# A layered conditional network on one core: raw differences, cut order and transfer order around the gated unit changed

## The reference, cut to what matters

```python
def lora_add(base, inp, A, B):
    t = jnp.einsum('bri,bni->bnr', A[0][ids], inp)
    return base + jnp.einsum('bor,bnr->bno', B[0][ids], t) * SCALE
gate = lora_add(x @ W_gate.T, x, A_gate, B_gate)
up   = lora_add(x @ W_up.T,   x, A_up,   B_up)
act  = silu(gate) * up
x    = x + lora_add(act @ W_down.T, act, A_down, B_down)
```

## Time and profile before

| | |
|---|---|
| median of 3 runs | 2181.67 us (2180.75 to 2182.43) |
| profiled execution | 2176.47 us, its span 2174.8 us |
| PE busy in the span | 2086.6 us (96%), 10432 matmuls |
| DVE, ACT, POOL busy | 1605.5, 969.6, 115.2 us |
| mean granted TensorE clock | 0.993 of full |
| 662 to 720 us (rows, half unit, start of unit 1, stage 0) | PE busy 45.00 of 58 us, clock 0.91 |
| 1165 to 1230 us (end of the units, first panels, stage 0) | PE busy 59.92 of 65 us, clock 0.97 |
| 1430 to 1480 us (half unit and start of unit 1, stage 1) | PE busy 47.39 of 50 us, clock 0.97 |
| 1915 to 1975 us (end of the units, first panels, stage 1) | PE busy 53.42 of 60 us, clock 0.97 |

### The profile page before, as it was taken

How to read it: one execution, slowest core, us unless ns; L and a number is a source line. 1 busy time by engine, 2 the same in 40 slices (tenths; PEclk the granted TensorE clock), 3 DMA queues, 4 the chain that set the end, 5 groups by cost and what they waited for, 6 DMA issues and landing times.

```text
span 2174.8 us, 34185 instructions
## 1 busy us (share of the span) xinstructions
PE 2086.6 (96%) x10432; PEld 1774.5 (82%) x10432; DVE 1605.5 (74%) x2132; ACT 969.6 (45%) x1268; POOL 115.2 (5%) x167
## 2 busy tenths in 40 slices
PE   2998999999998899999999999999999999999998
PEld 2998888888887788888888888888888888877887
DVE  7777999999997887878785347367878787743433
ACT  2222888788885334343333225333334333323222
POOL 3110000000005230000000000000000000000000
PEclk9999999999999999999999999999999999999999
DMA  5999999989997673434334995443333333364543
GB/s 194 377 360 358 351 358 362 342 339 353 362 349 257 189 206 102 109 95 110 92 96 148 272 247 178 164 135 93 108 97 105 100 100 105 89 199 154 184 155 126
DMA packets 258274, 441.49 MB, mean 203 GB/s; under 512 B 146934, under 2 KB 151222, under 8 KB 238006
## 3 DMA queue, kind: packets, MB, share of 16 engines
q1 hardware_dynamic: 245206, 410.79, 57.3%
q0 software_dynamic: 10848, 29.91, 4.2%
q10 hardware_dynamic: 2176, 0.26, 0.1%
HBM read 400.74 MB, written 63.73 MB: 214 GB/s over the span
## 4 chain that ended last, share of the span: by engine, by line
PE 84%; DVE 7%; DMA 3%; issue 2%; ACT 2%; POOL 1%; DVEq 0%; SPq 0%; ACTq 0%; POOLq 0%
PE ps L1937 19%; PE ps L1938 19%; PE ps L1939 19%; PE ps L1881 6%; PE ps L1883 6%; PE ps L1882 6%; PE ps L1857 3%; PE ps L2016 2%; PE ps L2015 2%; PE ps L1890 1%; DMA wraw<-in_wd 1%; PE ps L2051 1%; DMA wraw<-picked_bd 1%; PE ps L2052 1%; DMA W<-in_w 1%
## 5 line engine op out<-in xcount | busy, mean ns | idle before, releaser
L1937 PE MATMUL ps<-rows,oph 128*128 128x512 f32 x1196 | 468.9, 392 | 10.6 <-ACT tmp L855 8.4
L1938 PE MATMUL ps<-rows,oph 128*128 128x512 f32 x1196 | 468.1, 391 | 0.0
L1939 PE MATMUL ps<-rows,opl 128*128 128x512 f32 x1196 | 466.3, 390 | 0.0
L1389 DVE TENSOR_TENSOR wl<-W,wh 128x2048 fp32r<-128x2048 f32 x152 | 342.2, 2283 | 5.8 <-ACT wh L791 5.7
L1473 DVE TENSOR_TENSOR tmp<-ps,tmp 128x512 f32<-128x512 f32 (+1 forms) x340 | 234.1, 689 | 131.8 <-PE ps L2016 66.9
L1470 DVE TENSOR_TENSOR wdl<-wraw,wdh 128x1024 fp32r<-128x1024 f32 x92 | 112.5, 1224 | 274.1 <-ACT wdh L855 274.1
L791 ACT ACTIVATE wh<-W 128x2048 fp32r<-128x2048 f32 x152 | 290.5, 1914 | 37.3 <-DMA W<-in_w 34.0
L1937 PE MATMUL ps<-acb_h,wdh 128*128 128x512 f32 (+1 forms) x736 | 282.1, 383 | 12.4 <-DVE wdl L1470 7.0
L1938 PE MATMUL ps<-acb_l,wdh 128*128 128x512 f32 (+1 forms) x736 | 281.0, 382 | 0.0
L1939 PE MATMUL ps<-acb_h,wdl 128*128 128x512 f32 (+1 forms) x736 | 280.8, 382 | 0.0
L1937 PEld LDWEIGHTS ps<-rows,oph 128*128 128x128 f32 x1196 | 225.9, 189 | 55.6 <-issue 7.7
(11 more groups left out here) (222 smaller groups left out, 2831.9 us busy)
## 6 DMA issues: line engine op xcount, KB each, us to landing
W<-in_w SPq DMA_DIRECT2D x152, 1024.0 KB, 6.1
raw<-in_wgu SPq DMA_DIRECT2D x168, 256.0 KB, 2.7
wraw<-in_wd SPq DMA_DIRECT2D x84, 512.0 KB
toep<-kpad SPq DMA_DIRECT2D x32, 1024.0 KB, 8.8
lraw<-picked_b SPq DMA_DIRECT2D x88, 256.0 KB, 4.0
raw<-kept_acts SPq DMA_DIRECT2D x88, 256.0 KB, 3.4
kept_acts<-tmp SPq DMA_DIRECT2D x84, 256.0 KB, 2.3
picked_b<-in_lora_b POOLq DMA_DIRECT2D x32, 352.0 KB, 4.6
```

Of the source, the lines that this page charges most:

```text
L1389: V.tensor_tensor(out=wl[:, c], in0=W[:, c], in1=wh[:, c].bitcast(F32), op=ALU.subtract).then_inc(w_lo, 1)
L1937: mm(to, lhsT=wh, rhs=mh, start=start, stop=False)
L1938: mm(to, lhsT=wh, rhs=ml, start=False, stop=False)
L1939: return mm(to, lhsT=wl, rhs=mh, start=False, stop=stop)
```

## The change

1. POOL keeps the raw difference T3; T4 (`second_half(0)` minus T2) goes to DVE, behind the first `ranks_part`.
2. Stage 0, ACT: an empty sigmoid loads the activation table early; `ranks_hi(0)`, then the cut of A11, stand before `ranks_projected`, both of whose halves now run together; T3 is cut next. DVE correspondingly: T4, the cut of T2, `ranks_lo(0)`, the cut of A11, then both `ranks_cut`.
3. Both stages, in the half unit: `copy_p1`, `ranks_hi` and `down_ranks_hi` of unit 1 go ahead of the last cuts; the halves' products, `ranks_lo(1)` and `down_ranks_lo(0)` stand ahead of the cuts of T3, S3, A22, T4, S4 on DVE. Unit 1 is written out ahead of the loop, which starts at 2 now.
4. Both stages, `first_panels`: of panel 1, output 0 goes ahead of `project_down`, and outputs 1 to 3 instead of 0 to 5 stand before the wait for `td_added`; outputs 4 to 7 come after outputs 6 and 7 of panel 0.
5. SP: the residual rows come in four parts of 512 KB, at panels 5, 9, 13, 17 of the stage's first tile and 4, 8, 12, 16 of its second, instead of 2 MB at panel 4 and 2 MB at panel 6 of the first; the 36 row loads come two a panel at panels 4 to 21 instead of three a panel at 8 to 19. A wait for the third sum is added ahead of a quarter's load.

```diff
+            def load_residual(tile, part):
+                if part == 0:
+                    sp.wait_ge(unit_step, at_step(tile // 2, FT, 1))
+                    sp.wait_ge(x_saved[tile // 2], 16)
+                mine = slice(2 * part, 2 * part + 2)
...
-                    if at == 4:
-                        load_residual(2 * st)
-                    if at == HALF_AT:
-                        load_residual(2 * st + 1)
-                    if 8 <= at < 20 and st == 0:
-                        load_rows(1, (at - 8) // 3, (at - 8) % 3)
+                    if at in (5, 9, 13, 17):
+                        load_residual(2 * st, at // 4 - 1)
+                    if at < 22 and st == 0:
+                        load_rows(1, 2 * (at - 4))
+                        load_rows(1, 2 * (at - 4) + 1)
...
-            pool.wait_ge(t_raw, 2)
-            pool.wait_ge(ap_lo, 2 * GR)
-            pool.tensor_tensor(out=by_rows(LO[T4]), in0=second_half(0), in1=by_rows(LO[T2]),
-                               op=ALU.subtract).then_inc(t4_raw, 1)
...
+                copy_p1(st, 1)
+                ranks_hi(st, 1)
+                down_ranks_hi(st, 0, at_step(st, 0, AD))
                 act.wait_ge(evict, emptied(st, 0, V_ACT0))
                 copy(ahl[0:HALF, 0, 0], s0[0:HALF]).then_inc(act_hi, 1)
...
                 ranks_part(st, 0)
+                if st == 0:
+                    dve.wait_ge(t_raw, 2)
+                    sub(by_rows(rraw[LO[T4]][:]), rows_in(0, 1), by_rows(rraw[LO[T2]][:])).then_inc(t4_raw, 1)
+                    dve.wait_ge(t4_raw, 1)
+                    operand_lo(T2, rraw[LO[T2]][:], 11)
+                    ranks_lo(st, 0)
                 ranks_part(st, 1)
+                if st == 0:
+                    lo(st, 1, A11)
                 ranks_cut(st, 0)
...
-                        project_down(st, FT - 1)
                     else:
-                        down(tile, tile * NPAN + 1, 1, range(6))
+                        down(tile, tile * NPAN + 1, 1, (0,))
+                        project_down(st, FT - 1)
+                        down(tile, tile * NPAN + 1, 1, (1, 2, 3))
                 pe.wait_ge(td_added, 2 * st + 2)
                 down(tile, tile * NPAN, 0, (6, 7), start=True).then_inc(panel_done, 1)
-                down(tile, tile * NPAN + 1, 1, (6, 7)).then_inc(panel_done, 1)
+                down(tile, tile * NPAN + 1, 1, (4, 5, 6, 7)).then_inc(panel_done, 1)
```

More of the change, by code:

```diff
@@ L347, in build @@
         tile_done = sem("tile_done")
-        resid_in = sem("resid_in")
+        resid_in = [sem(f"resid_in{j}") for j in range(2)]
         d_added = sem("d_added")
@@ L510, in next_quarters @@
                 load_quarter(2, u, 2)
+                sp.wait_ge(sums, u * 4 + (st * 4 * (FT - 1) + 3))
                 for k, slot in ((0, A11), (1, A12), (3, A22)):
@@ L981, in half_unit @@
             def half_unit(st):
-                if st == 0:
-                    act.wait_ge(x_saved[1], 16)
-                for i in (A11, S2, A12, S1):
+                if st:
+                    hi(st, 1, A11)
+                for i in (S2, A12, S1):
                     hi(st, 1, i)
@@ L1004, in half_unit @@
                 copy(ahl[0:HALF, 1, 0], s1[0:HALF]).then_inc(act_hi, 1)
-                ranks_hi(st, 1)
+                for i in (S3, A22):
+                    hi(st, 1, i)
+                if st == 0:
+                    operand_hi(T4, rraw[LO[T4]][:])
+                hi(st, 1, S4)
             def unit(st, u):
-                copy_p1(st, u)
-                down_ranks_hi(st, u - 1, at_step(st, u - 1, AD))
+                if not isinstance(u, int):
+                    copy_p1(st, u)
+                    down_ranks_hi(st, u - 1, at_step(st, u - 1, AD))
                 hi(st, u + 1, A11)
@@ L1090, in _ @@
             operand_hi(T2, rraw[LO[T2]][:])
+            nc.scalar.activation(tick[:, 1:2], tick[:, 0:1], ACT.Sigmoid)
             act.wait_ge(x_saved[0], 16)
-            act.wait_ge(t3_raw, 1)
             for st in range(NST):
@@ L1095, in _ @@
                     act.wait_ge(cleared, 2 * st + 2)
-                ranks_projected(st, 0)
-                if st == 0:
+                    ranks_projected(st, 0)
+                    ranks_hi(st, 0)
+                    ranks_projected(st, 1)
+                else:
                     act.wait_ge(t4_raw, 1)
-                ranks_hi(st, 0)
-                ranks_projected(st, 1)
+                    ranks_hi(st, 0)
+                    act.wait_ge(x_saved[1], 16)
+                    hi(st, 1, A11)
+                    act.wait_ge(t3_raw, 1)
+                    ranks_projected(st, 0)
+                    ranks_projected(st, 1)
+                    operand_hi(T3, rraw[LO[T3]][:])
                 half_unit(st)
-                with act.Fori(1, FT - 1) as one:
+                unit(st, 1)
+                with act.Fori(2, FT - 1) as one:
                     unit(st, one)
@@ L1635, in half_unit @@
                 add_weights(st, 1)
-                for i in range(4):
+                if st:
+                    lo(st, 1, A11)
+                for i in (S2, A12, S1):
                     lo(st, 1, i)
-                if st == 0:
-                    dve.wait_ge(t4_raw, 1)
-                    operand_lo(T2, rraw[LO[T2]][:], 11)
                 dve.wait_ge(sig, st * 2 * FT + 1)
@@ L1743, in add_tile @@
                 if o == 0:
-                    dve.wait_ge(resid_in, (tile + 1) * 16)
+                    dve.wait_ge(resid_in[tile % 2], (tile // 2 + 1) * 64)
                 if o < LT - 1:
@@ L1776, in _ @@
                 ranks_part(st, 0)
+                if st == 0:
[4 more added lines that the diff above has]
+                    ranks_lo(st, 0)
                 ranks_part(st, 1)
+                if st == 0:
+                    lo(st, 1, A11)
                 ranks_cut(st, 0)
-                ranks_lo(st, 0)
+                if st:
+                    ranks_lo(st, 0)
                 ranks_cut(st, 1)
                 half_unit(st)
-                with dve.Fori(1, FT - 1) as one:
+                unit(st, 1)
+                with dve.Fori(2, FT - 1) as one:
                     unit(st, one)
```

66 lines of the change are left out of this document (26 added, 40 removed).

## The result

| | before | after |
|---|---|---|
| median | 2181.21 us, 4 runs (2178.2 to 2182.43) | 2157.51 us, 4 runs |
| ratio | | 0.9897, 95% interval 0.988 to 0.9913 |
| profiled execution, its span | 2176.47, 2174.8 us | 2157.1, 2155.4 us |
| PE busy | 2086.6 us (96%) | 2081.8 us (97%) |
| DVE, ACT, POOL busy | 1605.5, 969.6, 115.2 us | 1610.5, 967.6, 101.7 us |

One run of the changed kernel took 7494.94 us, for a reason the record does not show, and is left out of the ratio (the 2157.51 counts it); the other three lie between 2156.46 and 2157.91 us, with a median of 2157.10. The change is faster by 1.0%. The forecast was 2161.5 us (2156 to 2171): the direction and the range held.

A forecast was written before the change was run, and what follows sets the result against it. PE, busy 96% of the span, was taken as the bound, so only its gaps could be won: 4.6 + 2.6 + 3.2 + 9.8 = 20.2 us off 2181.67 gave 2161.5 us, range 2156 to 2171.

The forecast's parts named there:

- Panel 2 at B and D, 1.6 and 1.6: Down stage: reordered first-panel outputs start panel 2 1.6 us earlier in each stage, 0.5 us of its 1.80 us wait staying.
- B and D: Places where PE waits in the first panels of tile 0 and of tile 2, ahead of panels 2 and 7.
- Panel 7, 9.8 together: Tiles 0 and 2: residual loads cause waits of 3.00 and 3.97 us; removing them gains 9.8, about 0.6 coming back.
- The row loads, ahead at panels 4 to 7, cost nothing.: Tile 0: row loads are free while two take SP less than a panel's 5.45 us.
- the 3.4: SP's queue: two row loads take 3.4 us, 1.7 each, from three that took 5.18 in the steady stretch.
- Place A, 4.6: Unit 1 of stage 0: gain of 6.3 us less 1.6 for the clock, 4.6; bounds 1.5 and 6.3.
- V: Point in unit 1 where bank C's rank matmuls start after waiting for v_u3; forecast at 722.3 in stage 0.
- T3 gets its turn at 682.1 as before: Stage 0: POOL's T3 difference waits for DVE's two-input run to end; DVE's T4 then waits until 686.7.
- Rival 3: Port served in order of start: T3 over by 677, T4 unhindered, V 3 us earlier, 2158.5 us; chance 0.04.
- The wait of 5.79 us for ACT is replaced by one of 4.8 us for DVE: Unit 1 of stage 0: the copy_p1 wait goes, and a 4.8 us wait comes four blocks further on, before V.
- Place C, 2.6: Unit 1 of stage 1: V at 1472.3 against 1474.92, gain 2.6 us; bounds 1.0 (clock falls) and 4.4 (no wait).
- with a wait of 1.8 us left, inside what left the clock alone: Stage 1, before V: PE still waits 1.8 us, a length taken not to lower the clock.

The follow-up runs named there:

- e3: Changed kernel with the order of the first two panels' outputs as before the change; 2164.26 us, ratio 0.9922 to the kernel before.
- e4: Changed kernel with residual loads at panels 4 and 6 of each stage's first tile and row loads three a panel at 8 to 19; 2169.06 us, ratio 0.994.
- e1: Changed kernel with each stage's residual asked for at panels 4 and 6 of its first tile again, row loads as changed; 2173.94 us, ratio 0.9966.
- e2: Changed kernel with the row loads three a panel at panels 8 to 19 again, residual still in parts; 2171.14 us, ratio 0.9957.
- e9: Changed kernel with unit 1's products on DVE ahead of unit 2's sums and low parts, ACT's sigmoid ahead of unit 2's first cuts; 2158.13 us, ratio 0.9899.
- e6: Changed kernel with copy_p1 of unit 1 put back behind the last cuts of the half unit on ACT; 2157.64 us, ratio 0.9893.
- e5: Changed kernel, but POOL waits for the second of DVE's raw differences of tile 1 before starting T3; 2161.13 us, ratio 0.9915.
- e8: Changed kernel with the T4 raw difference back on POOL, all else in the new order; 2159.22 us, ratio 0.9912.
- e12: Changed kernel with T3's raw difference on DVE too, and the second mask product ahead of T2's low part; 2155.96 us, ratio 0.9901.

## Why the prediction was right, and where it was not

**Panel 2 at B and D, 1.6 and 1.6.** Right in size and cause; the after trace has 0.42 and 0.33 us left where 0.5 was said, and e3 takes back 1.6 and 1.6.

**Panel 7, 9.8 together.** Right in cause and nearly in size (its own terms, 4.0, 5.0 and 0.6, add up to 9.6): with the clock B gave 4.5 and D 6.1 beyond panel 2, 10.6 in all, and e4 takes back 10.6, though as 6.7 and 3.9. That it is the residual and not the rows is shown by tile 2 of e1, which takes back 6.1 at D. Panel 8 waits for 0.20 us; the 0.6 us that was to come back did not.

**"The row loads, ahead at panels 4 to 7, cost nothing."** For the changed kernel this held: no panel waits for `wraw`, and a pair cost SP 2.9 to 3.6 us at panels 9 to 13, counted with the delay of the weight load behind it, as the 3.4 had it, and mostly 1.1 later. SP's issues took about 4 us of a panel's 5.45 there, so the margin was real but not wide. That the 3.4 came out so well is partly luck: the 5.18 us behind it are the longest group after the first, the others took 3.4 to 4.4. But as a statement on row loads it is wrong. Their place is worth 13 us once the residual is in parts (e2), which the forecast had nowhere; it counted the spread over 18 panels as free, and it is what makes the parts work.

**Place A, 4.6.** It gave 3.8, by a sum that held but for one step. The forecast's times are of the execution before, which is 1.06 us behind the changed kernel's at 605; with that added, PE stood before V at 718.6 (said 717.4) and V came at 723.3 (said 722.3), with a wait of 4.72 us for DVE (said 4.8). The failed step is "T3 gets its turn at 682.1 as before". T3 started first, took 4.63 us instead of 14.55 and held DVE for 4.4 us at 671, so PE lost 2.15 us at 681, which the sum had nowhere. DVE got most of this back, since no T3 stood ahead of T4 any more: T4 started at 687.2 in those terms, said 686.7. PE's rank matmuls at 697 came 1.0 us late and so did V. In e9, where T3 did get its turn as before, they came at 697.3 in those terms, said 697.2: the rest of the sum was right, up to there. (The items of the next sum, down to 713.4, add up to 16.0 and not to 16.2 us.)

Rival 3 had the port's order right (chance 0.04) and T3's end (676.7 in those terms, said 677), but not its gain of 3 us: it took it that T3 would cost DVE nothing. That the measured 2157.5 us lies nearer to its 2158.5 than to the forecast is chance. The spread of A over the five executions with these same units and the same turn at the port (changed kernel, e1 to e4) is 0 to 1.9 us, more than the 0.8 that A was off.

**`copy_p1`.** "The wait of 5.79 us for ACT is replaced by one of 4.8 us for DVE" was right to 0.1 us. It should have been thought to its end: if DVE sets V, the move itself gains nothing, as e6 shows.

**Place C, 2.6.** It gave 0.8 in the profiled execution, and the failed step is "with a wait of 1.8 us left, inside what left the clock alone". The wait is 1.76 us, V came at 1461.42, and the clock was 0.67 over the next 5 us (the second window above), that is at the lower level for part of the time. But e5 has a wait of 1.76 us at the same instruction and a clock of 1.00 behind it:

```profile
1468.46:1472.46 4.00, 4.00 (x21) 3.48 (x22) 3.96 (x7) 1.03 (x2) 0.00 (x0) 1.00 0.08 27
```

as have e1, e2, e3, e4 and e8 after 1.70 to 1.87 us, and e12 after 1.46. Without the fall C gives 0.8 + 1.6 = 2.4, where the forecast had 2.6. So the term was right for these seven executions and wrong for the changed kernel's own; the bound of 1.0 "clock falls" was for that case, and it was undercut by 0.2.

**The total.** 18.4 us from the four places where 20.2 was said; with 1.6 for C's clock 20.0. The medians differ by 23.7 us, the ratio's interval says 19 to 26. The remainder is not from these places, and the executions' 5 us spread ahead of 605 us is large enough to hold it; no run tells more. So the cause of most of the gain, at B and D, was forecast and is shown; at A the size was near by terms of which one was wrong; and that the total stayed in the range, 1.5 us above its lower end, owes something to that spread.

## What to carry to other kernels

Before moving an operation that PE is seen to wait for, ask which engine sets the time of the next wait: here a wait of 5.8 us for ACT was DVE's total work in disguise, and moving it by itself gained nothing that the medians show (e6). Taking work from DVE, or moving it behind the point where PE needs it, gained 1 to 2 us at A each and 7.9 together (with two smaller steps); only the latter shows in the median. A two-input POOL operation of this size that got the port cost DVE 4.2 to 4.4 us where DVE itself needs 2.3, so "free" help from POOL is dear wherever DVE is the bound. Large loads that are not urgent go in small parts between the urgent ones, and the other loads of the same queue have to be spread with them: here either half of that change alone was 13 to 16 us worse than the pair, and neither half only 10.6.
